# Attention stage: VectorE's batches written out; row statistics taken in the fourth unit of the batch in front, rows loaded in its third

## What is computed

```python
x = x + 0.5 * ffn(layernorm(x))      # 4096 rows of 512, top 4 of 32 experts
x = x + attention(layernorm(x))      # 8 batches of 512 rows, 16 heads of 32
x = x + 0.5 * ffn(layernorm(x))

qkv = x @ Wqkv.T + b_qkv             # attention, per batch
scores = q @ k.T * scale + alibi_bias, causal
p = softmax(scores)
out = (p @ v) @ Wout.T + b_out
```

## Time and profile before

| | before |
|---|---|
| median of three runs | 2665.93 us |
| lowest, highest | 2659.95, 2668.38 us |
| the profiled execution, whole | 2671.62 us |
| its span, first to last instruction | 2669.8 us |
| mean granted TensorE clock | 0.958 |
| TensorE, VectorE, ScalarE, GpSimd busy | 2407.5, 1328.3, 1516.3, 1337.0 us |

### The profile page before, as it was taken

The page is one execution under the profiler, slowest core; times in us unless marked ns, Lnnn a source line. Parts: engine busy times, 40 slices in busy tenths (PEclk is TensorE's granted clock), DMA queues, the critical chain, the costliest instruction groups (busy, mean ns, idle before and its releaser), DMA issues. The chain is left out here.

```text
span 2669.8 us, 67005 instructions
## 1 busy us (share of the span) xinstructions
PE 2407.5 (90%) x12341; PEld 1828.1 (68%) x12342; DVE 1328.3 (50%) x3662; ACT 1516.3 (57%) x3779; POOL 1337.0 (50%) x1296
## 2 busy tenths in 40 slices
PE   0699999999999569998998999995899999999998
PEld 0578888888888445665656656563688888888886
DVE  8545555555533335546455464542455555555432
ACT  5666666666655325445454454542566666666654
POOL 4255555555655214444454444534455555666554
PEclk9899999999999779998999989997899999999999
DMA  9577877787710323333333333331677777878500
GB/s 314 181 183 171 182 180 175 175 189 189 179 22 0 91 73 89 95 86 109 98 91 96 91 108 97 88 85 50 175 173 190 183 169 171 193 178 193 115 0 1
DMA packets 181222, 348.97 MB, mean 131 GB/s; under 512 B 47143, under 2 KB 98215, under 8 KB 179986
## 3 DMA queue, kind: packets, MB, share of 16 engines
q0 software_dynamic: 76416, 148.62, 26.6%
q1 hardware_dynamic: 93456, 189.91, 24.6%
q10 hardware_dynamic: 11266, 9.61, 1.3%
HBM read 228.24 MB, written 117.96 MB: 130 GB/s over the span
## 5 line engine op out<-in xcount | busy, mean ns | idle before, releaser
L559 PE MATMUL f_psg<-f_wh,f_xh 128*128 x1280 | 535.9, 419 | 5.4 <-DVE f_idle L720 5.3
L559 PE MATMUL f_psg<-f_wh,f_xl 128*128 x1280 | 505.4, 395 | 0.0
L559 PE MATMUL f_psg<-f_wl,f_xh 128*128 x1280 | 503.0, 393 | 0.0
L507 POOL DMA_INDIRECT f_xg<-xn_rows,f_it x320 | 350.7, 1096 | 119.5 <-issue 94.7
L515 POOL DMA_INDIRECT x_rows<-f_ob,f_it x160 | 255.5, 1597 | 296.6 <-ACT f_ob L656 160.0
L515 POOL DMA_INDIRECT out<-f_ob,f_it x160 | 255.6, 1598 | 287.2 <-ACT f_ob L656 129.1
L1403 DVE CUSTOM_DVE_ANT_0 a_psa<-a_psa,cst 128x384 f32<-128x384 f32 (+3 forms) x512 | 249.8, 503 | 258.1 <-PE a_psa L1121 239.8
L1276 ACT ACTIVATE a_pt<-a_psb 128x256 f32<-128x256 f32 (+3 forms) x512 | 213.3, 437 | 207.1 <-PE a_psb L1184 202.0
L656 ACT ACTIVATE f_ob<-f_pso,f_wcol 128x512 f32<-128x512 f32 x320 | 220.5, 689 | 193.5 <-PE f_pso L573 193.3
L1019 POOL TENSOR_TENSOR a_pt<-a_pt 128x256 f32<-128x256 f32 (+2 forms) x384 | 266.9, 732 | 119.0 <-PE a_psc L1149 113.4
L727 DVE TENSOR_TENSOR f_xl<-f_psx,f_xh 128x512 fp32r<-128x512 f32 x320 | 221.5, 692 | 137.6 <-ACT f_xh L637 137.6
(11 more groups left out here) (194 smaller groups left out, 4326.7 us busy)
## 6 DMA issues: line engine op xcount, KB each, us to landing
f_wraw<-w_in SPq DMA_DIRECT2D x128, 768.0 KB, 6.0
a_stq<-a_qk SPq DMA_DIRECT2D x128, 144.0 KB
a_stk<-a_qk SPq DMA_DIRECT2D x128, 144.0 KB
r_xt<-x_in SPq DMA_DIRECT2D x8, 1024.0 KB, 14.0
xn_rows<-r_xt SPq DMA_DIRECT2D x8, 1024.0 KB, 14.7
a_xt<-x_rows SPq DMA_DIRECT2D x8, 1024.0 KB, 5.2
a_x<-x_rows SPq DMA_DIRECT2D x8, 1024.0 KB, 5.5
out<-a_x POOLq DMA_DIRECT2D x8, 1024.0 KB, 5.4
```

What stands on the lines that cost most here:

```text
L507: g.indirect_dma_start(xg[:, n % XB, :], None, xn_d, bass.IndirectOffsetOnAxis(it[:, n:n + 1], 0), bounds_check=tok_max, oob_is_err=False) ...
L559: mm = pe.matmul(psg[:, j, :], x[:, j, k, :], w[:, cols], start=(k == 0 and n == 0), stop=(k == DC - 1 and n == 2))
```

## The change

Four edits in `attend`.
- VectorE runs all eight batches written out, with no loop.
- `means` leaves unit 0 of the batch in front. The statistics of batch b+2 are taken in unit 3 of batch b, so one unit before the unit 0 in which they were taken until now. Those of batch 1 stay in unit 0 of batch 0. They keep their places behind maxima 5, 7, 9 and 12.
- SyncE's `load_x(b + 2)` stands in unit 2 of batch b, behind that unit's `stacks`; until now `load_x(b + 1)` stood at the head of unit 0 of batch b. Batch 1's load stands in front of the loop.
- SyncE's loop covers batches 0 to 5; batches 6 and 7 are written out and load nothing.

```diff
                 def batch(b):
-                    last = whole(b)
+                    last = whole(b) and b == B - 1
                     for g in range(NG):
-                        if g == 0 and not last:
-                            load_x(b + 1)
                         if not (last and g >= 2):
                             stacks(b * NG + (g + 2), (g + 2) % NG)
+                        if g == 2 and not whole(b):
+                            load_x(b + 2)
                         if g == 1:
                             residual(b)
...
                 sp.wait_ge(s_wl, len(pieces))
-                with sp.Fori(0, B - 1) as b:
+                load_x(1)
+                with sp.Fori(0, B - 2) as b:
                     batch(b)
+                batch(B - 2)
                 batch(B - 1)
...
-                            if g == 0 and i in STATS_AT and not last:
-                                means(b + 1, *STATS_AT[i])
+                            ahead = 1 if b == 0 and g == 0 else 2 if g == 3 and b + 2 < B else 0
+                            if ahead and i in STATS_AT:
+                                means(b + ahead, *STATS_AT[i])
...
-                batch(0)
-                with v.Fori(1, B - 1) as b:
+                for b in range(B):
                     batch(b)
-                batch(B - 1)
                 for t in range(TB):
                     finish(B - 1, t)
```

## The result

| | before | after |
|---|---|---|
| median of three runs | 2665.93 us | 2708.03 us |
| lowest, highest | 2659.95, 2668.38 | 2706.25, 2708.92 |
| the profiled execution, whole | 2671.62 | 2708.03 |
| its span | 2669.8 | 2706.0 |
| mean granted TensorE clock | 0.958 | 0.948 |

The account below looks back on a forecast made before the run. TensorE was taken to set the time. Six units 3 at 13.5 us cost 81, less gains of 39, net 42 us more: 2714 us for the profiled execution, 2708 us against the median, range 2675 to 2732.

Parts of the forecast that it names:

- VectorE's wait for the rows: Unit 3, batches 0 to 5: VectorE reaches the first statistics before the loaded rows land and waits 6.4 us.
- TensorE's wait by it: Unit 3: the ninth score tile starts late because the seventh maximum is late; 6.7 us in each of six units.
- statistics in unit 3 and their fall: Unit 3: three more statistics, the wait and the aggregates cost 1.9 us, the clock fall behind them 2.9 us.
- units 0 without both: Batches 1 to 6 without loop return and statistics: 41.45 us per unit 0, 248.7 in all, a gain of 29.5 us.
- units 1 and 2: Batches 1 to 6: without the 1.66 us wait before unit 1 they take 258.6 us, a gain of 9.5.
- The load: SyncE issues it half a microsecond behind unit 2's twenty stack transfers; it lands 5.2 us later, after VectorE wants it.
- The clock: Unit 3: TensorE's clock falls behind the wait for rows, 2.0 us, and again behind the statistics, 2.9 us.
- The way back: VectorE's loop return before unit 0: 3.09 us idle, TensorE waits 1.80 us; writing the batches out removes it.
- rival C: Unit 0's starting idle time is not the loop's and stays when written out: +55 us, 2721 us; chance 0.05.
- The statistics' 1.9 us: Unit 3: added time per unit for three more statistics, the wait and the aggregates, taken from a range of 1.7 to 2.3.
- Rival A: Unit 3: the wait comes but the clock stays up or falls where free: +13, 2679 us; chance 0.82 together with the forecast.
- rival B: Unit 3: rows arrive in time, only statistics and a fall are paid: 2656 us, or 2638 without a fall; chance 0.10.

Follow-up runs that it names:

- experiment 1: Kernel after with the load of batch b+2 issued ahead of unit 2's twenty stack transfers, not behind them: 2658.39 us, ratio 0.9972.
- experiment 4: Kernel after with batch b+2's statistics and aggregates taken in unit 3 behind the negated maxima, load still late: 2634.77 us, ratio 0.9895.
- experiment 6: Load-first kernel (experiment 1) with the statistics spread behind the 2nd, 4th, 7th and 9th maxima, aggregates behind the 14th: 2627.56 us, ratio 0.9849.
- Experiment 5: Kernel after with the load issued inside unit 2's series, behind fourteen of the twenty stack transfers: 2689.72 us, ratio 1.0077.
- experiment 2: Kernel before with VectorE's eight batches written out and nothing moved: 2657.27 us, ratio 0.9964.
- experiment 3: Kernel after with VectorE's loop back over batches 1 to 5, load and statistics left where the change put them: 2727.93 us, ratio 1.0232.
- experiment 8: Kernel before with VectorE's batches written out and statistics left in unit 0 but spread to other maxima, load at its old place: 2634.17 us, ratio 0.9884.

## Why the prediction came out

It had 2708 us, and the median is 2708.03. That it fits to the microsecond is luck. The working gave 42 us more for the profiled execution, 2714, and took off 5.7 because the profile of before lay that much above its median. The profile of after is at its own median, 2708.03, so the two profiled executions differ by 36 us and not 42; the 6 us that the terms were too high for these two and the 5.7 us taken off cancel. From the first to the last marker it is 37.9 us. Term by term, for the six batches:

| term | predicted | measured | from |
|---|---|---|---|
| VectorE's wait for the rows | 6.3 to 6.9, 6.4 taken | 6.0 to 7.4, mean 6.4 | kernel after |
| TensorE's wait by it | 6.7 | 6.3 to 7.6, mean 6.7 | kernel after |
| with the clock behind it | 8.7 | 8.5 | units 3, after less experiment 1 |
| statistics in unit 3 and their fall | 4.8 | 2.65 in unit 3 + 1.85 in unit 0 = 4.5 | experiment 1 |
| units 0 without both | 248.7 in all | 248.6 | experiments 4, 6 |
| units 1 and 2 | 258.6, 9.5 gained | 259.5, 8.6 gained | kernel after |
| all that unit 3 costs, its part in the next unit 0 too | 13.5 | 12.8 | kernel after |

- **The load** was the deciding step, and it was right in place and size: it goes out 0.4 us behind the series (0.5 said), and lands in 5.4 us (5.2 said).
- **The clock.** The first fall came in each of the six units 3, the second behind the statistics in five (in batch 1 the first lasted on into the values: a mean of 0.70 over its unit 3). Experiment 5 shows that the size of the first did not hang on the length of the wait from 2.9 us on, as I had half assumed when I gave it up to 3 us.
- **The bookkeeping of unit 0.** I wrote that units 0 would take 41.5 us and put the second fall into unit 3, and gave 30 to 35 us for that. Most of that fall lies behind the marker: units 0 took 42.7 to 43.7 and units 3 30.6 to 31.7. The sum of both, 74.9 said, was 73.4 to 75.2.
- **Units 1 and 2** came out right in sum by two errors that cancel: units 1 took 23.8 us on the mean where 23.2 was said, and units 2 19.5 where 20.0 was said, as one in six fell and not every second.
- **The way back** was real (rival C is out): gone in experiment 2, back in experiment 3. Its price in the prediction, rival C's 1.8 us and some clock, is not settled: 0.8 to 3.0 us by the medians of experiment 2, some 5 by those of experiment 3, where the clock fell for longer behind it.
- **The statistics' 1.9 us** was taken as a price of their being in a unit. Experiment 6 shows that it was the price of the block behind the 13th maximum. Right sum, reason only half right: the prediction had named the block and its wait, and did not ask whether the wait would go with another placing in the same unit.
- **Rival A**, that the clock stays up, did not happen; **rival B**, the rows in time, is what experiment 1 is: said 2656 with a fall in unit 3, measured 2658 with a fall behind the statistics in all six.

The change thus brought 28 us in units 0 to 2 of batches 1 to 6 and paid 67 us in six units 3 for it, 51 of them for a load queued behind transfers that nobody needed sooner (experiment 1 puts it in front of them at no loss). The Trainium skill, "DMA: Bandwidth & Descriptors", section "Issuing engines are not separate DMA queues", says that the sequencer's time to initiate a DMA is usually small relative to the DMA itself. For one transfer this agrees (0.38 us against 5.4). For the load at the end of a series it does not help, and the measurement decides: the series keeps SyncE for over 13 us (twenty issues of 0.6 to 0.8 us, from 1276.4 to 1289.9 in batch 2), more than twice the load's own time.

## What to carry to other kernels

A prefetch is timed by its place in the issuing queue: count the issues in front of it, add its landing, and compare that with the moment at which the in-order consumer arrives. Here each microsecond that it fell short made the unit about 1 us longer, and falls of TensorE's clock came on top. Before work is moved out of a busy unit, look for the one place in it where pieces stand in a row: spreading them in place gained here as much as moving them (2634 us in experiment 8, 2635 in experiment 4). On an engine that feeds TensorE, look at what a hardware loop's way back costs: here 3.0 to 3.3 us of VectorE's time, of which TensorE waited for 1.7 to 2.0.

## What was not expected of the hardware

- TensorE waits of only 1.58 to 1.99 us were followed, in 43 of 46 cases in batches 0 to 6 of all the kernels here, by a fall of the granted clock to the 1.2 GHz level, for 3 to 10 us; two of the three exceptions are in batch 4 of the kernel before. Waits under 1.0 us were followed by one seldom: experiment 4, whose longest in batches 1 to 6 was 0.96 us, had a granted clock of 1.00 in each of their 24 units; experiment 6 with the same longest wait had falls in four of them. What makes the difference is open.
- Written-out VectorE code came with fewer instruction transfers than its loop: 67 on q14 in the kernel before and 51 in experiment 2, 65 in experiment 3 and 52 in the kernel after, so about three for each way back. Each of the nine ways back shows as 3.0 to 3.3 us of idle time by "issue". That these transfers are the idle time fits, but was not tested.
